# Last stage of a two-layer transformer kernel: a chunk's activations are rounded before the next activation, and first-layer products run as two halves of 256 columns

## The reference

```
probs = softmax(xf @ router_w + router_b)
tw, ti = top_k(probs, 8);  tw = tw / sum(tw)
for e in range(64):                       # D=256, H=64
    h = silu(xf @ W1[e] + B1[e]) @ W2[e] + B2[e]
    acc += cw[:, None] * h                # cw: tw where ti == e, else 0
shared = sum over 2 shared MLPs: silu(xf @ SW1 + SB1) @ SW2 + SB2    # H=512
out = x + acc + shared
```

## Time and profile before

| | |
|---|---|
| median of 3 runs | 3064.24 us (3055.07 to 3066.49) |
| the profiled execution | 3059.81 us, its span 3058.1 us |
| instructions | 50413 |
| PE busy | 2517.8 us (82%) |
| PEld, DVE, ACT, POOL busy | 72%, 58%, 44%, 27% |

### The profile page before, as it was taken

The page is one execution under the profiler, slowest core; times in us unless marked ns, Lnnn a source line. Parts: engine busy times, 40 slices in busy tenths (PEclk is TensorE's granted clock), DMA queues, the critical chain, the costliest instruction groups (busy, mean ns, idle before and its releaser), DMA issues. The chain is left out here.

```text
span 3058.1 us, 50413 instructions
## 1 busy us (share of the span) xinstructions
PE 2517.8 (82%) x18511; PEld 2196.2 (72%) x18511; DVE 1787.3 (58%) x3152; ACT 1330.8 (44%) x2053; POOL 810.6 (27%) x1143
## 2 busy tenths in 40 slices
PE   1988888885229999973677778877999999999999
PEld 1777676774229999972466566666888888988988
DVE  5555555544228888866877777726744544444444
ACT  0444444542017776753333334333444444444444
POOL 3444444401430000014566564541000000000000
PEclk9799999987559999995789899998999999999999
DMA  2000000004137676755555454404422222222222
GB/s 83 1 2 2 2 1 2 2 1 140 58 134 242 228 242 226 239 177 149 140 126 133 130 135 120 133 28 142 131 93 83 87 83 87 83 83 82 92 75 87
DMA packets 191373, 312.26 MB, mean 102 GB/s; under 512 B 28308, under 2 KB 100184, under 8 KB 191192
## 3 DMA queue, kind: packets, MB, share of 16 engines
q1 hardware_dynamic: 179112, 272.01, 29.2%
q0 software_dynamic: 12080, 37.76, 3.7%
HBM read 269.84 MB, written 39.85 MB: 101 GB/s over the span
## 5 line engine op out<-in xcount | busy, mean ns | idle before, releaser
L2143 DVE TENSOR_TENSOR e_h_lo<-e_h,e_h_hi 128x512 fp32r<-128x512 f32 x320 | 221.5, 692 | 476.0 <-ACT e_h_hi L2219 475.9
L2205 ACT ACTIVATE e_h<-e_h_ps,e_b 128x512 f32<-128x512 f32 x320 | 219.9, 688 | 494.8 <-PE e_h_ps L2284 476.7
L2300 PE MATMUL e_y_ps<-e_w_hi,e_h_hi 128*128 128x256 f32 x1280 | 363.7, 284 | 15.2 <-DVE e_h_lo L2143 15.1
L2300 PE MATMUL e_y_ps<-e_w_hi,e_h_lo 128*128 128x256 f32 x1280 | 358.6, 280 | 0.0
L2300 PE MATMUL e_y_ps<-e_w_lo,e_h_hi 128*128 128x256 f32 x1280 | 357.8, 280 | 0.0
L2300 PEld LDWEIGHTS e_y_ps<-e_w_hi,e_h_hi 128*128 128x128 f32 x1280 | 240.2, 188 | 40.0 <-DVE e_h_lo L2143 24.9
L2284 PE MATMUL e_h_ps<-e_yT_hi,e_w_hi 128*128 128x512 f32 x640 | 257.3, 402 | 1.5 <-ACT e_h L2205 0.6
L402 DVE TENSOR_REDUCE a_top<-a_ring 128x2 f32<-128x1024 f32 (+3 forms) x256 | 202.8, 819 | 89.6 <-PE a_ring L603 88.7
L2284 PE MATMUL e_h_ps<-e_yT_hi,e_w_lo 128*128 128x512 f32 x640 | 253.7, 396 | 0.0
L2284 PE MATMUL e_h_ps<-e_yT_lo,e_w_hi 128*128 128x512 f32 x640 | 253.3, 396 | 0.0
L2300 PEld LDWEIGHTS e_y_ps<-e_w_lo,e_h_hi 128*128 128x128 f32 x1280 | 240.5, 188 | 13.2
(11 more groups left out here) (360 smaller groups left out, 6914.3 us busy)
## 6 DMA issues: line engine op xcount, KB each, us to landing
e_w<-in_w SPq DMA_DIRECT2D x78, 1024.0 KB, 5.4
e_spread<-share_store SPq DMA_DIRECT2D x512, 128.0 KB, 2.8
a_keys<-rows_store SPq DMA_DIRECT2D x128, 256.0 KB, 5.1
a_queries<-rows_store SPq DMA_DIRECT2D x86, 256.0 KB, 4.5
a_running_hidden<-rows_store SPq DMA_DIRECT2D x42, 256.0 KB, 4.4
sorted_x<-zeros POOLq DMA_DIRECT2D x10, 1024.0 KB, 16.9
e_xs<-sorted_x SPq DMA_DIRECT2D x39, 256.0 KB, 5.0
sorted_y<-e_ys POOLq DMA_DIRECT2D x39, 256.0 KB, 5.7
```

What stands on the lines that cost most here:

```text
L2143: dve.tensor_tensor(h_parts[q % 2][1][:, :], h[:, q % 2, :], h_parts[q % 2][0][:, :], ALU.subtract).then_inc(h_lo.sem, h_lo.tick())
L2205: act.activation(h[:, q % 2, :], h_ps[q % 2][:, :], ACT.Silu, bias=b1[:, c:c + 1]).then_inc(h_ready.sem, h_ready.tick())
L2300: last = pe.matmul(y_ps[n][:, 0:D], h_parts[q % 2][a][:, n * P:(n + 1) * P], w2[b][:, c, :], start=(q == 0 and m == 0), stop=(q == CH - 1 ...
```

## The change

Two edits, both in `experts1_phase`. ACT's list is reordered: for every chunk `silu(q)` is followed by its own `high(q)`. And `up` runs its six products twice, once for each half of 256 tokens, so that it issues 12 products with 256 columns and 12 weight loads; the semaphore is raised once, after the last. The arithmetic is the same.

```diff
@@ -2224,15 +2224,11 @@
             for i in range(B):
                 more = i + 1 < B
-                silu(i, 0)
                 for q in range(CH):
-                    if q < CH - 2:
-                        silu(i, q + 1)
+                    silu(i, q)
+                    if q == CH - 1 and more:
+                        high_tokens(i + 1)
                     high(i, q)
-                    if q == CH - 2:
-                        silu(i, q + 1)
-                        if more:
-                            high_tokens(i + 1)
...
@@ -2279,9 +2275,10 @@
...
-                ops = [(w1[a][:, k, c * P:(c + 1) * P], yT[b][:, k, :]) for k in range(KC) for a, b in TERMS]
-                for m, (l, r) in enumerate(ops):
-                    last = pe.matmul(h_ps[q % 2][:, :], l, r, start=(m == 0), stop=(m == len(ops) - 1))
+                for cols in (slice(0, S // 2), slice(S // 2, S)):
+                    ops = [(w1[a][:, k, c * P:(c + 1) * P], yT[b][:, k, cols]) for k in range(KC) for a, b in TERMS]
+                    for m, (l, r) in enumerate(ops):
+                        last = pe.matmul(h_ps[q % 2][:, cols], l, r, start=(m == 0), stop=(m == len(ops) - 1))
                 last.then_inc(up_done.sem, up_done.tick())
```

## The result

| | before | after |
|---|---|---|
| median, both kernels on one chip | 3058.62 us (6 runs, 3045.88 to 3066.49) | 3027.32 us (6 runs, 3026.17 to 3031.56) |
| ratio | 1 | 0.9901, 95% interval 0.9877 to 0.9925 |
| profiled execution, its span | 3059.81, 3058.1 us | 3026.40, 3024.6 us |
| PE products of the program | 18511 | 20431 |

The changed kernel is faster by 1.0%, 31 us by the medians.

What follows compares the result with a forecast made beforehand. PE was taken as the bound, busy 118.84 of 120.57 us a sequence. Reordering at -18.3 us and halves at +4.5 gave -13.8 us, taken as 3049 us, range 3034 to 3060.

Steps and rivals of the forecast that it cites:

- The bound and the reach of edit 1: Last stage: PE bounds; rounding ahead of the next activation removes PE's waits, -18.3 us of at most 25.7.
- Exponentials: Exponentials in 7 sequences: PE's 0.93 us stall before down(34) goes, with a reserve of 0.34.
- The rival that had this stall stay: The exponentials' stall stays in another place: about 7 us given back, 3057; chance 0.16.
- Next tokens: Sequence's end: up(0)'s 0.63 us stall mostly goes, since silu(39) starts some 0.2 late; 0.14 kept.
- the forecast's second sign of being wrong: The prediction is wrong if a PE wait of 0.3 us or more still comes in each later sequence.
- First sequence: First sequence, where DVE sets the pace for a while: 6.6 of 10.9 us of stalls left, 4.4 gained.
- Edit 2: up in halves: 1920 products and 1920 weight loads more on PE, 0.014 us for each of 320 chunks, +4.5 us.
- the forecast's own sign of being wrong: The prediction is wrong if a step of PE is over 0.119 or under 0.117.
- a rival at 0.08: Halves change PE's pace upward in the last stage, to 0.1135 a step: 3032 or 3016; chance 0.08.
- the first case: Ups alone go at 0.1135 a step: 16.6 us less than forecast, 3032; the pace rival's chance is 0.08.
- the argument against it: Against the quicker pace: the earlier mixture also shows 0.1178 for the same stream, so width doesn't decide.

Runs made afterwards that it cites:

- e1: Changed kernel with up's six full 512-column products as before, so ACT's new order alone; 3037.66 us, ratio 0.9932 to the kernel before, stage 949.5 us.
- e2: Kernel before with up in halves of 256 columns, ACT's old order kept; 3048.44 us, ratio 0.9974 to the kernel before, stage 960.7 us.
- e4: PE's stream alone (last stage's activation-to-low-part work and token-weight transfers left out of the changed kernel, h constant), up with six full products; 3030.53 us, stage 942.1.
- e10: Like e3, but up has five terms in halves, then the last as one full 512-column product; 3020.87 us, stage 932.6.
- e3: Changed kernel without the last stage's activation, multiplication, rounding, low part and token-weight transfers, h constant, up in halves; 3022.22 us, stage 931.1.
- e5: Like e3, but with one h_ps and one h_parts buffer for all chunks; 3027.73 us, stage 931.6.
- e6: Like e3, but the first term of up is one full 512-column product, the other five in halves; 3006.70 us, stage 917.8.
- e8: Like e3, but the last half product of each up is repeated, thirteen in all; 3075.78 us, stage 978.0.
- e13: Like e3, but one half product of each up is left out, eleven remaining; 2981.64 us, stage 893.2.
- e14: Like e3, but two half products of each up are left out, ten remaining; 2959.73 us, stage 865.4.
- e16: Like e3, but up has five full 512-column products first and the last term in halves; 3048.62 us, stage 941.0.

## Why the prediction was right on one edit and wrong on the other

- *The bound and the reach of edit 1.* Right. PE stays the bound, and the forecast of 18.3 us measured 18.6 in e1's stage; the first sequence gained 4.2 (128.1 to 123.9, first `down` to first `down`) for 4.4 forecast, each later one 2.2 to 2.3 for 2.32. The rule behind it, that a wait costs its idle time plus the lateness and the restart that the row leaves out, gave the right sum here.
- *Exponentials.* The stall of 0.93 is gone, and the reserve was thinner than forecast. The changed kernel's timeline there:

```profile
2419.32 1.28 ACT L2194 ACT_TABLE_LOAD   x1
...
2421.05 1.28 ACT L2205 ACT_TABLE_LOAD   x1
...
2422.35 0.69 ACT L2205 ACTIVATE e_h<-e_h_ps,e_b 128x512 f32<-128x512 f32 x1
...
2424.46 0.69 DVE L2143 TENSOR_TENSOR e_h_lo<-e_h,e_h_hi 128x512 fp32r<-128x512 f32 x1 [0.70 <-ACT e_h_hi L2219]
...
2425.37 0.28 PE L2297 MATMUL e_y_ps<-e_w_hi,e_h_hi 128*128 128x256 f32 x1
```

  The low part ends at 2425.15 and `down` starts at 2425.37 without a wait: 0.22 less the hand-over of 0.05, so 0.17 for the forecast's 0.34. The chain took 0.08 longer than forecast, and PE, whose blocks are quicker, was due 0.09 earlier. The rival that had this stall stay was 0.2 us away in each sequence.
- *Next tokens.* Right in direction, a little short in size. The changed kernel's timeline from the end of `up(39)` to `up(0)`, which answers to the earlier trace rows:

```profile
2433.72 0.28 PE L2297 MATMUL e_y_ps<-e_w_hi,e_h_hi 128*128 128x256 f32 x1
...
2434.16 0.67 ACT L2205 ACTIVATE e_h<-e_h_ps,e_b 128x512 f32<-128x512 f32 x1
...
2435.50 1.28 DVE L2116 TENSOR_TENSOR e_yT_lo<-e_yT_next,e_yT_hi 128x512 fp32r<-128x512 f32 x2
...
2436.43 0.28 PE L2297 MATMUL e_y_ps<-e_w_hi,e_h_lo 128*128 128x256 f32 x1
...
2436.84 0.39 PE L2281 MATMUL e_h_ps<-e_yT_hi,e_w_hi 128*128 128x256 f32 x1
```

  `silu(39)` starts 0.44 behind its `up`, 0.24 late as forecast, but `up(0)` comes 0.41 behind the last product of `down(38)` where a step is 0.12: it is 0.29 late and keeps that much of the 0.63, not 0.14. From `silu(39)` to `up(0)` it is 2.68 again, and the forecast's own figures had said so: with `silu(39)` 0.2 later than 0.20 behind its `up`, 0.20 + 0.2 + 2.68 is 0.26 over the 2.82 that are due. Of the six boundaries that makes less than 1 us. The load ahead of `up(0)` still waits 0.30 to 0.33 in each later sequence, so the forecast's second sign of being wrong, a wait of 0.3 or more there, came too.
- *First sequence.* Right, with its new waits. `up` waits for an activation at 2083.10 and 2087.49, 0.76 and 1.26, at the very start, where 2.3 was forecast; the four waits for the low part, 2.2 in all, and one of `up`, 0.9, lie between 2110 and 2200, where 2.3 and 1.7 were forecast. (The forecast's figures hold lateness and restart besides the idle time, so like is not quite compared with like.)
- *Edit 2.* **This is the step that failed: "All blocks of the last stage go at the slow pace, so I take that."** It put twelve halves at 0.1178 each, 1.414 for a block, and kept the downs at 1.41. In the runs nearly half of the steps of both kinds go at 0.1134 (0.40 and 0.48 in after), which is also the forecast's own sign of being wrong, a step under 0.117. An `up` takes (1.42 + 1.37) / 2 = 1.395 on the mean and a `down` (1.42 + 1.36) / 2 = 1.39, where before had 1.40 and 1.41: 0.025 less a chunk, 1.0 a sequence, 8 in all, against 7.4 and 7.3 measured for e2 and for after over e1. The forecast had +4.5, so the term was off by 12 us, and by sign. The slow pace had been a property of the stream that the edit replaces, and I read it as one of the stage. I had the other pace in the earlier trace rows and left it as a rival at 0.08; that rival gave two cases, ups alone all quick (16.6 less than forecast) and downs too. Its direction was right and neither case came: part of both kinds is quick, 12 less than forecast. That the median, 3027, lies near the first case's 3032 is luck, since 5 us of the gain are not the stage's. Nor did the argument against it hold: that the same stream shows both paces in the earlier trace rows left both open for the new one.
- *The remaining 5 us* between 25.9 in the stage and 31 in the medians are not explained by the changed code. The profiled executions show that the stages ahead vary by more than that. With the forecast's edit 2 at its measured size the sum is -18.3 - 7.4 = -25.7, which is the stage's 25.9.
- The Trainium skill (TensorE: Matmul & The Clock Gate, Back-to-back issue gap) gives a single product a fixed gap of about 2.5 ns over its columns, by which halves can only cost. The traces agree at the slow pace alone: two halves are 235.6 ns and a full product of e4 233.4 on the mean, 2.2 less. At the quick pace two halves are 226.8 and a full product behind ten mostly quick halves, in e10, 226.7, so nothing is added. The larger difference, 8.8 ns for two halves, is that between the paces. The same page (LDWEIGHTS) puts the load of 128 columns at 107 ns, as an estimate by its formula, which would fit behind a half's 113.4. No row shows the 107, since the loads' rows in the trace are 0.19 us long and overlap; but the loads did not come into the open: with 1920 more of them the sequence is shorter.

## What to carry to other kernels

On a bounding engine price an edit by its step, start to start, and if the trace shows two levels of it for the same instruction, take both as possible for the new stream and give each its chance, above all when the edit changes the very stream that shows the one level. Where such a level can't be predicted, try neighbouring forms: here one product left whole at the start of each block took another 9.7 us off the stage, where the split had taken 7.3, though whole executions are too uneven to show the 9.7. A reordering that only moves waits off the path could here be worked out to 0.3 of 18.6 us, with every wait counted with its lateness and restart.

## What the runs showed of the hardware that was not expected

- A pair of weight load and 256-column product (fp32r, clock 1.00) takes 113.4 or 117.8 ns from start to start, in long unbroken runs of one or the other. The two paces alternate in the same way without the waits for h, the work on h and the second buffer (e3, e5), and their shares do depend on how many products a chunk has and on where a 512-column one stands (e6, e8, e10, e13, e14, e16): from none to 0.88 of the steps were quick. A 512-column product has more than one pace too, 226.7 ns behind quick halves in e10 and 233.4 in e4.
- One product more in a chunk cost 46.9 us in the stage (e8 over e3), where 320 slow steps are 37.7; one fewer gave 37.9 (e13 under e3), which is 320 steps of 118, and two fewer 65.7 (e14 under e3), where 640 slow steps are 75.4. The cost of a product is not a constant.
